# A sandwich of two attention layers on one core: the experts' product ahead of the first turned block, and the attentions' constants and first loads

## The reference, cut to what matters

```
x = x + _layernorm(_L0_attn_ref(_layernorm(x), ...))   # RWKV scan
x = x + _layernorm(_L0_ffn_ref(_layernorm(x), ...))    # 32 experts, each on its 8 best tokens
x = x + _layernorm(_L1_attn_ref(_layernorm(x), ...))   # rotary attention, 16 heads of 16
x = x + _layernorm(_L1_ffn_ref(_layernorm(x), ...))    # attention, 8 heads of 32, weights sliced
```

## Time and profile of the kernel before

| | |
|---|---|
| median of 3 runs | 6439.22 us (6426.44 to 6443.73) |
| the profiled execution | 6442.2 us, its span 6440.4 us |
| PE busy | 5802.5 us (90%) |
| DVE busy | 4966.1 us (77%) |
| ACT busy | 4062.1 us (63%) |
| POOL busy | 2210.5 us (34%) |
| TensorE's granted clock, mean | 0.925 |

### The profile page before, as it was taken

How to read it: one execution, slowest core, us unless ns; L and a number is a source line. 1 busy time by engine, 2 the same in 40 slices (tenths; PEclk the granted TensorE clock), 3 DMA queues, 4 the chain that set the end, 5 groups by cost and what they waited for, 6 DMA issues and landing times. The chain is left out here.

```text
span 6440.4 us, 114697 instructions
## 1 busy us (share of the span) xinstructions
PE 5802.5 (90%) x39242; PEld 2644.4 (41%) x39242; DVE 4966.1 (77%) x6641; ACT 4062.1 (63%) x7304; POOL 2210.5 (34%) x1099
## 2 busy tenths in 40 slices
PE   5997766796999999999999999987999999999993
PEld 3443552353333333333333333343455555555532
DVE  5997520476999999899899999946777777777745
ACT  3775101121888888788888888854466666666660
POOL 2332100253000000000000000012599999999991
PEclk9998966786999999899999999976799999999995
DMA  4112668476333333333333333159211111111106
GB/s 148 49 46 69 182 221 297 129 229 137 48 50 49 49 50 50 48 50 49 47 52 52 51 51 51 28 161 321 57 40 40 40 40 40 41 40 40 40 6 213
DMA packets 372876, 548.16 MB, mean 85 GB/s; under 512 B 68736, under 2 KB 272832, under 8 KB 352608
## 3 DMA queue, kind: packets, MB, share of 16 engines
q1 hardware_dynamic: 359520, 524.12, 33.7%
q10 hardware_dynamic: 12800, 16.78, 0.7%
HBM read 351.36 MB, written 186.78 MB: 84 GB/s over the span
## 5 line engine op out<-in xcount | busy, mean ns | idle before, releaser
L687 DVE TENSOR_REDUCE at_NM<-at_MX 128x1 f32<-128x1024 f32 (+1 forms) x4096 | 3759.8, 952 | 606.3 <-PE at_MX L520 573.9
L629 ACT ACTIVATE at_PB<-at_S 128x512 f32<-128x512 f32 x6144 | 3281.9, 598 | 916.1 <-PE at_S L549 761.9
L520 PE MATMUL at_MX<-at_KT,at_QT 48*128 48x512 f32 (+1 forms) x6144 | 2388.8, 451 | 93.7 <-DMA at_VS<-v 66.8
L549 PE MATMUL at_S<-at_QT,at_KT 50*128 50x512 f32 (+1 forms) x6144 | 2340.5, 435 | 6.0 <-ACT at_PB L629 5.8
L560 PE MATMUL at_AV<-at_PB,at_VS 128*32 128x256 f32 (+1 forms) x20480 | 1865.2, 436 | 14.2 <-ACT at_AVS L637 13.3
L549 PEld LDWEIGHTS at_S<-at_QT,at_KT 50*128 50x128 f32 (+1 forms) x6144 | 1011.5, 188 | 927.2 <-issue 490.6
L520 PEld LDWEIGHTS at_MX<-at_KT,at_QT 48*128 48x128 f32 (+1 forms) x6144 | 1000.3, 191 | 595.1 <-DVE at_NM L687 405.7
L482 POOL TENSOR_TENSOR at_SUM<-at_SUM,at_PB 128x2048 f32<-128x2048 f32 x192 | 886.5, 4617 | 23.4 <-ACT at_PB L629 0.4
L560 PEld LDWEIGHTS at_AV<-at_PB,at_VS 128*32 128x32 f32 x20480 | 410.5, 108 | 968.7 <-ACT at_PB L629 823.9
L482 POOL TENSOR_TENSOR at_SUM<-at_PB 128x2048 f32<-128x2048 f32 x160 | 751.9, 4702 | 44.5 <-ACT at_PB L629 43.1
L455 POOL CAST at_NMR<-at_NMF 16x128 fp32r<-16x128 f32 x96 | 26.9, 280 | 1648.8 <-ACT at_NMF L642 1648.8
(11 more groups left out here) (198 smaller groups left out, 3849.0 us busy)
## 6 DMA issues: line engine op xcount, KB each, us to landing
moe_W<-in_w SPq DMA_DIRECT2D x64, 1024.0 KB, 10.8
at_QT<-qk SPq DMA_DIRECT2D x384, 128.0 KB, 5.3
at_KT<-qk SPq DMA_DIRECT2D x384, 128.0 KB, 6.9
qk<-r_HI SPq DMA_DIRECT2D x64, 512.0 KB, 6.7
qk<-r_LO SPq DMA_DIRECT2D x64, 512.0 KB, 6.2
at_VS<-v SPq DMA_DIRECT2D x96, 256.0 KB, 8.3
at_QT<-qk SPq DMA_DIRECT2D x96, 256.0 KB, 4.0
at_KT<-qk SPq DMA_DIRECT2D x96, 256.0 KB, 6.2
```

Of the source, the lines that this page charges most:

```text
L520: ins = nc.tensor.matmul(MX[r][:, a, :], QT[u][h:h + NQ, b * P:(b + 1) * P], KT[u][h:h + NQ, (c + a) * W:(c + a + 1) * W], start=True, sto ...
L549: nc.tensor.matmul(SP_[item(it, s, "score", t)[1]][:, :], KT[u][h:h + NQ + 2, kb * P:(kb + 1) * P], QT[u][h:h + NQ + 2, c * W:(c + 1) * W] ...
L629: nc.scalar.activation(PB[:, t % NPB, :], SP_[r][:, :], ACT.Exp, scale=scale).then_inc(exp_done, 1)
L687: nc.vector.tensor_reduce(NM4[:, b, c:c + 1], MX[r][:, :, :].rearrange("p a n -> p (a n)"), AX_X, ALU.max, negate=True).then_inc(ring_got, 1)
```

## The change

Two edits. In phase_rope PE issues `source(g + 1)` directly behind `turn(g)`, ahead of `turn_qk(g - 1, 0)`. In phase_attention the ones of buffers 0 and 1 are written by DVE (`set_ones`, `front_set`), those of 2 and 3 by POOL (`back_set`); SP waits for one buffer's ones before each unit's loads instead of for all four, and after unit 0's loads it waits until they have landed before it issues those of unit 1. PE no longer waits for the ones itself, except for ONES in the second attention (`ones_set`).

```diff
@@ phase_attention
-        const_ld, preset, ring_put, ... = (m.sem(n) for n in (
+        front_set, back_set, ones_set = (m.sem(n) for n in ("front_set", "back_set", "ones_set"))
+        const_ld, ring_put, ... = (m.sem(n) for n in (
+        def set_ones(eng, u):
+            for h in HALVES:
+                lo = (h + NQ) // 32 * 32
+                ins = eng.memset(KT[u][lo:lo + 32, :].bitcast(F32), 1.0)
+            return ins
@@ sync
-            sp.wait_ge(preset, NBUF)
...
             for it in range(3):
+                if it < 2:
+                    sp.wait_ge(front_set, it + 1)
+                else:
+                    sp.wait_ge(back_set, 2)
                 load(it, it)
+                if it == 0:
+                    sp.wait_ge(loaded[0], 16 * NLOAD)
             m_row(0, 0)
@@ gpsimd
-            for u in range(NBUF):
-                for h in HALVES:
-                    lo = (h + NQ) // 32 * 32
-                    ins = nc.gpsimd.memset(KT[u][lo:lo + 32, :].bitcast(F32), 1.0)
-                ins.then_inc(preset, 1)
+            for u in range(2, NBUF):
+                set_ones(nc.gpsimd, u).then_inc(back_set, 1)
             if not TWO:
-                pool.wait_ge(preset, NBUF)
-                nc.gpsimd.memset(ONES[:, :], 1.0).then_inc(preset, 1)
+                pool.wait_ge(back_set, 2)
+                nc.gpsimd.memset(ONES[:, :], 1.0).then_inc(ones_set, 1)
@@ tensor
-            pe.wait_ge(preset, NBUF if TWO else NBUF + 1)
+            if not TWO:
+                pe.wait_ge(ones_set, 1)
@@ vector
+            for u in range(2):
+                set_ones(nc.vector, u).then_inc(front_set, 1)
             for x in range(NMX):
                 maxima(0, 0, x)
@@ phase_rope, tensor
             for g in range(NGR):
                 turn(g)
+                if g + 1 < NGR:
+                    source(g + 1)
                 if g > 0:
                     turn_qk(g - 1, 0)
-                if g + 1 < NGR:
-                    source(g + 1)
```

More of the change, by code:

```diff
@@ L356, in phase_attention @@
             L = m.ps("L", [P, W])
-        const_ld, preset, ring_put, ring_got, nm_ready, nmr_split, nmr_ready, mrow = (m.sem(n) for n in (
-            "const_ld", "preset", "ring_put", "ring_got", "nm_ready", "nmr_split", "nmr_ready", "mrow"))
+        front_set, back_set, ones_set = (m.sem(n) for n in ("front_set", "back_set", "ones_set"))
+        const_ld, ring_put, ring_got, nm_ready, nmr_split, nmr_ready, mrow = (m.sem(n) for n in (
+            "const_ld", "ring_put", "ring_got", "nm_ready", "nmr_split", "nmr_ready", "mrow"))
         nmf_got, fo_got = (m.sem(n) for n in ("nmf_got", "fo_got"))
```

## The result

The changed kernel takes 6367.82 us (median of 4 runs, 6358.08 to 6377.16); the kernel before, run beside it, takes 6432.83 (4 runs, 6423.19 to 6443.73). The ratio is 0.9883, with a 95% interval of 0.9854 to 0.9912. The medians lie 65.0 us apart, the size that was forecast. By the ratio it is 75 us, with an interval of 57 to 94, and against 6439.2, on which the forecast of 6374 was built, it is 71. So the agreement to the microsecond is one of three readings, and the runs can't tell them apart; each part is read by itself.

A forecast was written before the change was run, and what follows sets the result against it. PE (90% busy) was taken as the bound, waiting in turn with DVE in phase_rope. Savings of 49 (phase_rope), 11.0 and 5.2 (attentions) and 0 (unit 0 alone) sum to 65 us: 6439.2 to 6374 us, range 6358 to 6404.

The forecast's parts named there:

- SP's first load 3.7 us after the start: First attention: two DVE memsets, back to back from the stage's start, let SP issue its first load at 3.7 us.
- being alone gives 0: First attention: unit 0's loads land in the same 15.5 us when held apart from unit 1's; gain 0.
- The wait was a loop of two engines, and the product stood in it: phase_rope: moving the product ahead makes PE the bound, period 15.15 us instead of 16.86; part worth 49 us.
- 29 of the 53 us come through the clock: phase_rope: 29.2 of 53.2 us come from PE's lower clock level going with its waits; 2 us charged back.
- The stores: phase_rope: ACT's values wait for stores two groups back; landings free up to 5.4 to 5.8 us, 2 us charged.
- rival (b): phase_rope: stores become the bound, landings of 7.5 us cost 1.7 us an iteration, 24 in all; 6396 us, chance 0.15.
- The constants: Attentions' start: DVE writing the first ones brings the first load 11.0 us earlier in the first, 5.2 in the second.
- rival c: Attentions: DVE's memsets queue behind Pool's at a shared port, 11 us less gain; 6385 us, chance 0.07.
- Unit 1 is not waited for: First attention: unit 1 lands 15.5 us later but has 22 us of cover before first use; cost zero.
- (a): phase_rope: the clock's lower level stays, 6389 us if half of the 29.2 us stays, 6403 if all; chance 0.15.
- (d): phase_rope: slower than before through late store landings, net loss from 12.1 us; 6470 us at 13, chance 0.02.
- (e): phase_rope: statistics still start behind the turned block, so only the attentions gain; 6423 us, chance 0.05.

The follow-up runs named there:

- e1: Kernel before with only phase_rope's new order, both attentions unchanged; 6377.88 us, ratio 0.9894.
- e3: Kernel before with 12 idle products on PE in place of its wait for DVE's last rope in phase_rope; 6429.78 us, ratio 0.9985.
- e6: Changed kernel with a 1.76 us memset on DVE ahead of the last rope in each inner iteration of phase_rope; 6413.99 us, one run.
- e5: Changed kernel with ACT's third copy of turned keys moved ahead of the first copy of values in phase_rope; 6362.86 us.
- e4: Changed kernel without SP's wait for unit 0's loads to land before issuing unit 1's; 6370.85 us.
- e11: e3 again, unchanged, on the kernel before, for a second profile; 6423.54 us.
- e12: e3 a third time, unchanged, on the kernel before, for another profile; 6437.65 us.

## Where the prediction was right and where it failed, point by point

The mechanisms of the two large parts were right. What failed are smaller terms of the sum, two steps above all: SP's first load 3.7 us after the start (it was 4.51, because DVE's late start and its gap between two memsets were put at nothing), and "being alone gives 0" (it gives some 0.7 us in the first attention and 0.5 in the second), of which the prediction said that it would be wrong if unit 0 landed faster alone. Everything outside of the three places was put at nothing too, apart from a spread in the range; the profiled spans differ by 11.4 us there.

- *The wait was a loop of two engines, and the product stood in it.* Right. The new period was 15.15 by the sum and 15.02 by the trace; the last iteration, bound by DVE, takes the 14.74 of the forecast's DVE loop to the hundredth (14.75 in e1), though the sum had charged 15.15 for it. Of the 0.13 between them, 0.11 is the stretch from first projection to turned x, 1246.27 - 1234.63 = 11.64 for 11.75 (the first projection takes 1.88 behind a turned block and took 1.98 behind the product), and 0.02 an overlap taken too small.
- *29 of the 53 us come through the clock.* Right, and shown from both sides by e3 and e6. The one slow spell of the first iteration is there: it takes 16.71, 1.7 over the period, where 2 were charged.
- *The stores.* The mechanism was named and the free landing put at 5.4 to 5.8 us; the trace has 5.2 without a wait and 6.3 with one. The charge, 2 us in all, was a mean of 0.15 over all iterations; it is four iterations of 0.7, 2.8 us by e5. The sign of rival (b), a wait of ACT's values for a DMA, is in the trace, but at a tenth of its 24 us. Likewise the idle before the statistics was to fall under 8 us and is 8.6.
- The misses of this part, 0.13 x 12 = 1.6 us of the period, 0.4 in the first iteration and 0.4 in the last (14.74 for 15.15) gained and 0.8 on the stores lost, leave 50.8 for 49.2.
- *The constants.* This step of the sum was mis-sized: "SP's first load 3.7 us" after the stage's start. It came after 4.51. DVE's memset was slightly shorter than taken (1.76 for 1.82), but DVE started 0.49 us behind POOL and stood 0.47 us between its two memsets, and neither had been counted. 11.0 became 10.2. In the second attention SP waits for one memset, so only the late start counts: the first load comes after 2.28 us for the forecast 1.9 (7.06 before), which is 4.8 less, and its loads take 9.65 us for 10.22. That 5.35 lies so near the forecast 5.2, and PE's idle of 29.23 so near the forecast 29, is luck: the late start and the faster loading are two misses of opposite sign. The prediction also took for granted that the memsets had to go to DVE; by its own row of 1.84 us a piece, POOL's first two would have ended at 3.7 us.
- *The shared port* (rival c, from the Trainium skill, Perfetto Trace Analysis, Optimizing Scalar/DVE Operations). No run here shows an effect: 1.76 us beside POOL and alone. That moving the memsets to DVE helped isn't shown by this: what SP no longer waits for is the other three buffers.
- *Alone is worth 0.* Wrong, by a small size: 0.5 us against before, 0.9 by e4, 0.7 by the means of all profiles. The wrong step was "the engines carried unit 0 first and nothing of the others before it". The loads took 15.5 us and the clean rate gave 14.0; the difference was left without a name, and about half of it went when the others were held back. By the ring order of the Trainium skill (DMA: Bandwidth & Descriptors, Queues, rings and completion order) it was 0 as well; the runs' 0.7 us decides.
- *Unit 1 is not waited for.* Right: behind unit 0's maxima no wait for a DMA appears.
- *Rivals.* (a) is out: the loop's clock is 0.99. (d) would have needed landings of 12.1 us. (e) is out by the idle before L2103.

## What to carry over

Where two engines wait for each other once an iteration, write down both loops, engine by engine, and ask which step can leave the longer one without being missed: here one exchanged pair of calls. A wait of 1.5 us on PE in each iteration cost more than itself again through the clock here (29 us for 14 waits), and a filling of idle products shows that share by itself, before anything is rebuilt; but judge it by the stage's length, since the total carries the clock's variation of other stages. When a loop gets shorter, look next at the landings that the engines wait for and at who is queued behind that wait: exchanging two steps there was free. And when work is moved to another engine and a wait is narrowed in one edit, ask of each alone what it is worth.

## What the runs showed of the hardware

- After a wait of 1.2 to 3.1 us in an otherwise dense loop one or two groups of PE's products take 3.1 to 3.8 us instead of 1.9, in some iterations and not in others. It came once behind 0.26 us in each of e3, e11 and e12, and in the changed kernel not behind 0.47.
- Stretches of 3 to 51 us at the lower level stand in the first attention, each behind a stop of PE of 1.5 to 3.1 us that nothing in the profile ends, with PE mostly busy from there on. They lie at about the same places (2490 to 2630 and 2990 to 3110 us, in e11 also at 2874 and in e11 and e12 from 3506 on), and their length changes from run to run. The attention's length spreads over 29 us in the profiles above, with the same work in it.
- DVE needs 1.76 us for a memset of 32 x 2048 floats and then stands 0.38 to 0.48 us before its next, and its first comes 0.49 us behind POOL's; POOL needs 1.77 to 1.84 and has no gap (four in 7.32 us).
- Unit 0's loads (1.83 MB), held apart from those of the next unit, let PE start some 0.7 us sooner after the first one (means of seven profiles each, 15.1 for 15.8 us).
